# Second feed-forward layer: its closing row normalisation moved from two passes of its own into the loop over batches

## The reference

```python
    def _L1_ffn_ref(x, Wr, br, W1, b1, W2, b2, gamma, beta):
...
        h = jax.nn.gelu(jnp.einsum('nd,edf->enf', xf, W1) + b1[:, None, :], approximate=False)
        y = jnp.einsum('enf,efd->end', h, W2) + b2[:, None, :]
        w_dense = jnp.zeros((N, E), x.dtype).at[jnp.arange(N)[:, None], top_i].add(top_w)
        out = jnp.einsum('ne,end->nd', w_dense, y).reshape(B, S, D)
        out = _layer_norm(out + x, gamma, beta)
        return out
...
    x = x + _L1_ffn_ref(_layernorm(x, axis=-1), L1_ffn_Wr, L1_ffn_br, L1_ffn_W1, L1_ffn_b1, L1_ffn_W2, L1_ffn_b2, L1_ffn_gamma, L1_ffn_beta)
    x = x + _L2_gnn_ref(_layernorm(x, axis=-1), adj, L2_gnn_W1, L2_gnn_b1, L2_gnn_W2, L2_gnn_b2)
```

## Time and profile before

| | |
|---|---|
| median of 3 runs | 6786.41 us (6783.37 to 6788.06) |
| the profiled execution: its own time | 6792.14 us |
| the profiled execution: span in the trace | 6790.4 us |
| busy over the span | PE 79%, DVE 67%, ACT 34%, POOL 1% |
| batch loop of the layer, 4878.4 to 5004.0 us of the span | PE busy all through |
| statistics of YB, 5004.0 to 5026.9 us | VectorE, one turn to ScalarE |
| closing pass over the batches, 5026.9 to 5082.8 us | VectorE alone |

### The profile page before, as it was taken

How to read it: one execution, slowest core, us unless ns; L and a number is a source line. 1 busy time by engine, 2 the same in 40 slices (tenths; PEclk the granted TensorE clock), 3 DMA queues, 4 the chain that set the end, 5 groups by cost and what they waited for, 6 DMA issues and landing times. The chain is left out here.

```text
span 6790.4 us, 109815 instructions
## 1 busy us (share of the span) xinstructions
PE 5355.4 (79%) x33047; PEld 3803.4 (56%) x33047; DVE 4564.6 (67%) x27007; ACT 2311.9 (34%) x7369; POOL 93.6 (1%) x128
## 2 busy tenths in 40 slices
PE   4666788888877769969899976993546699776999
PEld 4555566666666534446566653662333477554676
DVE  7888888888888853379999997775562333424333
ACT  1222222222222235449599881110110233201333
POOL 0000000000000000000000000000000000000000
PEclk9999999999999999969999987996778799876999
DMA  1000000000000000010000000000000000000000
GB/s 46 2 2 2 2 3 5 3 4 4 4 4 3 4 21 13 7 54 6 6 4 6 4 3 8 1 1 0 25 28 0 13 0 0 9 0 13 0 0 25
DMA packets 27823, 56.57 MB, mean 8 GB/s; under 512 B 6186, under 2 KB 16835, under 8 KB 25539
## 3 DMA queue, kind: packets, MB, share of 16 engines
q1 hardware_dynamic: 27330, 50.79, 2.2%
HBM read 38.20 MB, written 12.58 MB: 7 GB/s over the span
## 5 line engine op out<-in xcount | busy, mean ns | idle before, releaser
L2007 DVE SCALAR_TENSOR_TENSOR f_ACC<-f_yp,f_CG,f_ACC 128x128 f32<-128x128 f32 x1024 | 288.4, 344 | 461.6 <-DVEq L2005 461.6
L1952 PEld LDWEIGHTS f_yp<-f_W,f_hs 128*128 128x128 f32 x4096 | 490.0, 192 | 92.6 <-issue 91.8
L1886 PE MATMUL f_hp<-f_rows,f_W 128*128 128x512 f32 x1024 | 531.5, 602 | 5.1 <-ACT U L1896 3.0
L1054 ACT ACTIVATE e_XD<-e_X,e_scal 128x60 f32<-128x60 f32 x2048 | 527.5, 333 | 17.5 <-DVEq L918 15.7
L710 PE MATMUL h_small<-h_part,ones 128*128 128x2 f32 x1024 | 300.6, 363 | 294.3 <-DVE h_jd L579 198.4
L1983 ACT ACTIVATE f_hs<-f_hp,f_b 128x512 f32<-128x512 f32 x512 | 347.7, 685 | 539.7 <-ACTq L1982 539.7
L655 ACT ACTIVATE h_VW<-h_v,h_s 128x8 f32<-128x8 f32 (+3 forms) x512 | 154.8, 302 | 1082.6 <-DVE h_s L417 1082.6
L1942 PE MATMUL f_hp<-f_XT,f_W 128*128 x1024 | 484.4, 601 | 33.0 <-PEq L2236 33.0
L703 PEld LDWEIGHTS h_ax<-h_XM,h_parts 128*128 128x128 bf16 x11520 | 480.8, 114 | 40.9 <-issue 40.9
L1952 PE MATMUL f_yp<-f_W,f_hs 128*128 128x128 f32 x4096 | 493.5, 275 | 0.0
L710 PEld LDWEIGHTS h_small<-h_part,ones 128*128 128x128 f32 x1024 | 256.6, 311 | 415.0 <-DVE h_jd L579 287.6
(11 more groups left out here) (716 smaller groups left out, 11363.2 us busy)
## 6 DMA issues: line engine op xcount, KB each, us to landing
f_S<-in_f_W SPq DMA_DIRECT2D x64, 128.0 KB, 2.3
X<-in_x SPq DMA_DIRECT2D x1, 4096.0 KB, 16.3
held<-g0e_HL SPq DMA_DIRECT2D x16, 256.0 KB, 2.0
g_HL<-held SPq DMA_DIRECT2D x16, 256.0 KB, 2.8
f_W<-in_f_W SPq DMA_DIRECT2D x2, 2048.0 KB
spill<-f_xts SPq DMA_DIRECT2D x16, 256.0 KB, 2.0
f_rows<-spill SPq DMA_DIRECT2D x16, 256.0 KB, 2.7
f_W<-in_f_W SPq DMA_DIRECT2D x4, 1024.0 KB
```

What stands on the lines that cost most here:

```text
L1054: ins = nc.scalar.activation(XD[b][:, k, h, :], X[:, :], ACT.Identity, bias=scal[b][:, k, 2 * h:2 * h + 1])
L1886: nc.tensor.matmul(self.hp[s % 3][:, :], self.W1[:, e, j * P:(j + 1) * P], self.rows[:, g % 2, :], start=True, stop=True).then_inc(self.h_ ...
L1952: ins = nc.tensor.matmul(yp[:, u % 2, k, :], hs[:, u % 2, c, k * P:(k + 1) * P], W2[:, u * UC + c, :], start=(c == 0), stop=(c == UC - 1))
L2007: ins = V_.scalar_tensor_tensor(ACC[:, k, :], yp[:, u % 2, k, :], CG[:, k * E + e:k * E + e + 1], ACC[:, k, :], ALU.mult, ALU.add)
```

## The change

The two closing stages go. Their work moves into `chosen_experts`:

- VectorE takes bn_stats of a batch's four YB tiles directly after writing them, and adds beta to X's rows of the batch directly after the batch's input rows were normalised.
- Mean and variance become scales in two halves of 32 tiles, batches 0 to 7 (FIRST = 8) and 8 to 15. VectorE's `variance(half)` comes at the end of batch 7 and after the loop; ScalarE's `deviation(half)` (a square root) after its Gelus of batch 8 and after the loop; VectorE's `scales(half)` in batch 9 and after the loop.
- The normalising itself moves to ScalarE: `finished_rows(g)` makes YN = YB * rstd + bias with four instructions on 128x128, each with a scale and a bias that are one value per row. VectorE's `scaled_rows(g)` multiplies by gamma and adds to X. Both run nine batches behind (BEHIND = 9): batches 0 to 6 inside the loop's batches 9 to 15, and batches 7 to 15 after the loop.

```diff
+        YN = sb("YN", [P, 2, GT, D])
...
+        FIRST, BEHIND = 8, 9
+        halves = (slice(0, FIRST * GT), slice(FIRST * GT, T))
...
+                def finished_rows(g):
+
+                    act.wait_ge(bias_in, 1 if g < FIRST else 2)
+                    if g >= 2:
+                        act.wait_ge(x_out, g - 1)
+                    for k in range(GT):
+                        t = g * GT + k
+                        nc.scalar.activation(YN[:, g % 2, k, :], YB[:, t, :], ACT.Identity, scale=prstd[:, t:t + 1],
+                                             bias=pbias[:, t:t + 1]).then_inc(yn_full, 1)
+
+                def deviation(half):
+
+                    act.wait_ge(var_in, half + 1)
+                    nc.scalar.activation(psd[:, halves[half]], pv[:, halves[half]], ACT.Sqrt).then_inc(sd_out, 1)
...
+                    if g == FIRST:
+                        deviation(0)
+                    if g >= BEHIND:
+                        finished_rows(g - BEHIND)
+                deviation(1)
+                for g in range(B - BEHIND, B):
+                    finished_rows(g)
...
+                def variance(half):
...
+                    dve.wait_ge(stat_in, T // 2 * (half + 1))
...
+                def scales(half):
...
+                    dve.wait_ge(var_in, half + 1)
+                    dve.wait_ge(sd_out, half + 1)
...
+                def scaled_rows(g):
+
+                    dve.wait_ge(yn_full, GT * (g + 1))
+                    xs = X[:, g * GT:(g + 1) * GT, :]
+                    V_.tensor_tensor(YN[:, g % 2], YN[:, g % 2], gm[:, :].unsqueeze(1).broadcast_to([P, GT, D]), ALU.mult).then_inc(ch2, 1)
+                    dve.wait_ge(ch2, done.next())
+                    V_.tensor_tensor(xs, xs, YN[:, g % 2], ALU.add).then_inc(x_out, 1)
...
                     V_.tensor_tensor(ACC[:, a], XG[:, a], bp[:, a, 0:D].unsqueeze(1).broadcast_to([P, GT, D]), ALU.add).then_inc(y_free, 1)
+                    xs = X[:, g * GT:(g + 1) * GT, :]
+                    V_.tensor_tensor(xs, xs, bt[:, :].unsqueeze(1).broadcast_to([P, GT, D]), ALU.add).then_inc(ch2, 1)
+                    done.next()
                     dve.wait_ge(y_free, 3 * g + 1)
+                    if g == FIRST + 1:
+                        scales(0)
...
+                    for k in range(GT):
+                        V_.bn_stats(st[:, g * GT + k, :], YB[:, g * GT + k, :]).then_inc(stat_in, 1)
+                    if g == FIRST - 1:
+                        variance(0)
+                    if g >= BEHIND:
+                        scaled_rows(g - BEHIND)
+                variance(1)
+                scales(1)
+                for g in range(B - BEHIND, B):
+                    scaled_rows(g)
+                dve.wait_ge(x_out, B)
...
-        if post:
-            statistics(nc, C, signal, YB, mean, rstd, name + "_post")
...
-                                normalize(nc, dve, ch3, done, xg, YB, mean, rstd, g * GT, GT).then_inc(ch3, 1)
...
-                                V_.tensor_tensor(xg, xg, gm[:, :].unsqueeze(1).broadcast_to([P, GT, D]), ALU.mult).then_inc(ch3, 1)
...
-                                V_.tensor_tensor(xg, xg, bt[:, :].unsqueeze(1).broadcast_to([P, GT, D]), ALU.add).then_inc(ch3, 1)
...
-                                V_.tensor_tensor(xs, xs, flat(xg), ALU.add).then_inc(ch3, 1)
```

More of the change, by code:

```diff
@@ L2034, in chosen_experts @@
         ACC = sb("ACC", [P, 2, GT, D])
+        YN = sb("YN", [P, 2, GT, D])
+        st = sb("post_st", [P, T, 6])
+        pa, pb, pv, psd, pmean, prstd, pbias = (sb("post_" + k, [P, T]) for k in ("a", "b", "v", "sd", "mean", "rstd", "bias"))
         hp = bctx.enter_context(nc.psum_tensor(f"{name}_hp", [P, 2, FC, S], F32))
@@ L2090, in _ @@
                 done = Count()
+                def variance(half):
+                    hv = halves[half]
+                    dve.wait_ge(stat_in, T // 2 * (half + 1))
+                    me, mo, qe, qo = st[:, hv, 1], st[:, hv, 4], st[:, hv, 2], st[:, hv, 5]
+                    V_.tensor_tensor(pb[:, hv], me, mo, ALU.subtract).then_inc(ch2, 1)
+                    dve.wait_ge(ch2, done.next())
+                    V_.tensor_tensor(pa[:, hv], qe, qo, ALU.add).then_inc(ch2, 1)
+                    done.next()
+                    V_.scalar_tensor_tensor(pb[:, hv], pb[:, hv], 0.25, pb[:, hv], ALU.mult, ALU.mult).then_inc(ch2, 1)
+                    dve.wait_ge(ch2, done.next())
+                    V_.scalar_tensor_tensor(pv[:, hv], pa[:, hv], 1.0 / D, pb[:, hv], ALU.mult, ALU.add).then_inc(ch2, 1)
+                    dve.wait_ge(ch2, done.next())
+                    V_.tensor_scalar(pv[:, hv], pv[:, hv], EPS, None, ALU.add).then_inc(var_in, 1)
+                    V_.tensor_tensor(pmean[:, hv], me, mo, ALU.add).then_inc(ch2, 1)
+                    dve.wait_ge(ch2, done.next())
+                    V_.tensor_scalar(pmean[:, hv], pmean[:, hv], 0.5, None, ALU.mult).then_inc(ch2, 1)
+                    dve.wait_ge(ch2, done.next())
@@ new lines, in scales @@
+                def scales(half):
+                    hv = halves[half]
+                    dve.wait_ge(var_in, half + 1)
+                    dve.wait_ge(sd_out, half + 1)
+                    V_.reciprocal(prstd[:, hv], psd[:, hv]).then_inc(ch2, 1)
+                    dve.wait_ge(ch2, done.next())
+                    V_.tensor_tensor(pa[:, hv], prstd[:, hv], prstd[:, hv], ALU.mult).then_inc(ch2, 1)
+                    dve.wait_ge(ch2, done.next())
+                    V_.tensor_tensor(pa[:, hv], pa[:, hv], pv[:, hv], ALU.mult).then_inc(ch2, 1)
+                    dve.wait_ge(ch2, done.next())
+                    V_.tensor_scalar(pa[:, hv], pa[:, hv], -0.5, 1.5, ALU.mult, ALU.add).then_inc(ch2, 1)
+                    dve.wait_ge(ch2, done.next())
+                    V_.tensor_tensor(prstd[:, hv], prstd[:, hv], pa[:, hv], ALU.mult).then_inc(ch2, 1)
+                    dve.wait_ge(ch2, done.next())
+                    V_.scalar_tensor_tensor(pbias[:, hv], pmean[:, hv], -1.0, prstd[:, hv], ALU.mult, ALU.mult).then_inc(bias_in, 1)
@@ L2102, in _ @@
                         dve.wait_ge(y_free, 3 * g + 2 + c)
+                    for k in range(GT):
[9 more added lines that the diff above has]
+                dve.wait_ge(x_out, B)
+                dve.wait_ge(ch2, done.n)
 def experts(nc, C, X, w, name, F, func, by_batch=False, affine=False, post=False):
@@ L2366, in experts @@
         if by_batch:
-            chosen_experts(nc, C, signal, X, XT, XG, mean, rstd, w, b2, CBT, BS, index, share, YB, name, F, func)
+            chosen_experts(nc, C, signal, X, XT, XG, mean, rstd, w, b2, CBT, BS, index, share, YB, gm, bt, name, F, func)
         else:
             all_experts(nc, C, signal, X, XT, W1, W2, b1, b2, CB, name, F, func)
-        if post:
-            statistics(nc, C, signal, YB, mean, rstd, name + "_post")
[L2372 to L2383, removed]
-                                normalize(nc, dve, ch3, done, xg, YB, mean, rstd, g * GT, GT).then_inc(ch3, 1)
-                                dve.wait_ge(ch3, done.next())
-                                V_.tensor_tensor(xg, xg, gm[:, :].unsqueeze(1).broadcast_to([P, GT, D]), ALU.mult).then_inc(ch3, 1)
-                                dve.wait_ge(ch3, done.next())
-                                V_.tensor_tensor(xg, xg, bt[:, :].unsqueeze(1).broadcast_to([P, GT, D]), ALU.add).then_inc(ch3, 1)
-                                dve.wait_ge(ch3, done.next())
-                                xs = X[:, ds(g * GT, GT), :].rearrange("p a b -> p (a b)")
-                                V_.tensor_tensor(xs, xs, flat(xg), ALU.add).then_inc(ch3, 1)
-                                added = {**(added if b else {}), b: done.next()}
-                            dve.wait_ge(ch3, done.n)
-                            dve.sem_clear(ch3)
 GT = 4
```

5 lines of the change are left out of this document (4 added, 1 removed).

## The result

The changed kernel took 6714.85 us (median of four executions, 6713.43 to 6719.67), the kernel before 6787.24 (6783.37 to 6789.85).

A forecast was written before the change was run, and what follows sets the result against it. TensorE was taken to bound the batch loop and VectorE the closing pass. With the loop costing nothing more, 58.8 us off the profiled 6792.14 gave 6733.3, less 5.73 for the median: 6728 us, range 6717 to 6741.

The forecast's parts named there:

- the bound on the clock: Next stage's first matmuls: a shift in where TensorE's clock rises may change the time by 1.5 us either way.
- The layer's gain: Behind the loop: 78.8 us shrink as X's last row ends at 5024.0 instead of 5082.84, 58.8 us won.
- The table changes: ScalarE's square-root loads, 1.28 us each: covered in batch 9 by 0.3 us, on the path behind the loop.
- The rival by the Trainium skill: Each table switch adds a drain of some 1380 ns; 2.5 us more in all, 6730 us. Chance 0.06.
- ScalarE's group: Four 128x128 normalising instructions with two per-row operands: 1.26 us a group, one instruction every 0.29 us.
- the upper bound: ScalarE's four normalising instructions without overlap: 0.49 us each, 1.96 us a group, 4.5 us more in the tail.
- The rival in which ScalarE paces the tail: Nine groups behind the loop at 1.96 us each on ScalarE, 17.6 us, 4.5 more; 6732 us. Chance 0.13.
- The tail's total: From the loop's last row at 5004.02 to X's last row at 5024.0, with nine groups taking 13.1 us.
- VectorE as the loop's bound: VectorE above 7.62 us a batch, say 8.6 in the last seven; 7 us come back, 6735 us. Chance 0.07.
- The side of slower: TensorE's clock falls in the loop, a batch taking 15.2 us; with all 16 batches 6850 us. Chance 0.03.
- the rivals that made the gain smaller: ScalarE pacing the tail (6732 us, 0.13), a drain per table change (6730, 0.06), VectorE bounding the loop (6735, 0.07).

The follow-up runs named there:

- after_w8: Changed kernel with one VectorE operation of 8 columns (0.17 us) added behind its last row; executions 6717.60, 6717.81, 6733.90 and 6736.51 us.
- load_behind: Changed kernel with a one-column ScalarE copy, waiting for the variance, ahead of each square root; 6716.69, 6731.96, 6733.48 and 6735.54 us.
- rows_on_dve_warm: Changed kernel with YB's normalising moved from ScalarE to VectorE, plus six unread matmuls in each closure round of the fourth graph layer; 6716.76 us.
- after_d1: Changed kernel with one 128x512 VectorE operation (0.73 us) added behind its last row; 6732.26 us.
- after_again: The changed kernel itself, unedited, in four more executions; 6715.31, 6718.65, 6727.36 and 6729.58 us.
- no_scale: Changed kernel with the per-row scale left out of ScalarE's YN instructions, so its output is not the reference's; 6716.26 us.
- after_d2: Changed kernel with two 128x512 VectorE operations (1.46 us) added behind its last row; 6730.46 us.
- after_w1024: Changed kernel with one VectorE operation of 1024 columns (1.2 us) added behind its last row; 6734.50 us.
- quarters: Changed kernel with statistics in four parts of four batches instead of two of eight, finishing five batches behind instead of nine; 6723.53 us.
- before_d2: Kernel before with two 128x512 VectorE operations (1.46 us) added behind its closing pass; 6791.45 us.
- before_d3: Kernel before with three 128x512 VectorE operations (2.19 us) added behind its closing pass; 6793.15 us.

## Why the prediction was wrong

- **The step that failed** is the bound on the clock: "where the clock rises among them may shift by a few of them, so 1.5 us either way at the next stage", and, with it, that a later stage's length changes is something "which nothing here gives cause for". The runs showed a later stage whose TensorE clock takes one of two courses: its rounds took 65.9 us before and 51.2 after, 12.1 us of the kernel's time, and executions of one kernel lie up to 19 us apart (after_w8). 58.8 us off the kernel before gave 6728. In its eight executions the changed kernel had 6727.4 and 6729.6 on what by their times is the slow course, which is the forecast to within 2 us, and 6713 to 6720 on the fast one; that all four executions of the result were fast ones was luck. The sign was in the trace before: these rounds had a granted clock of 0.67, though TensorE waited only 2.35 us in each. The sum never asked what they would take at full clock, since no edit was near.
- **The layer's gain**: forecast 58.8, measured 59.7 (landmarks) and 59.3 (with the clock's choice gone). What was forecast of the loop held: 7.62 us a batch, the first weighted row on time. VectorE's busy time in the loop was 83.2 us, not "near 87": a batch's eight rows took 5.97 us together, not 6.6, since they overlap a little.
- **The table changes** cost nothing. In the loop the sum had the reload start when batch 9's first Gelu was due and make it 1.28 us late. It ran earlier, at 4941.42, while ScalarE would have waited for hp, and that Gelu came on time (4944.02, 7.62 us after the one before). Behind the loop the sum had the load on the path, 1.3 us too much: the last load ran at 4994.54, before the variance was out, and only the square root behind it waited for that, at 5000.47. load_behind puts the load on the path and gets 1.5 us. The earlier trace rows had shown it behind the wait; in that code a semaphore clear stands between the wait and the square root and in the changed kernel nothing does, but whether that is the reason was not tried. The rival by the Trainium skill (ScalarE: Activation LUTs, "What ACT_TABLE_LOAD costs", a drain of some 1380 ns with each switch) is not borne out here: 0.02 us from the load's end to the square root, and 0.01 us from the last Gelu of batch 8 (4938.98 + 0.69) to the load ahead of it (4939.68).
- **ScalarE's group** was put at 1.26 us and took 1.64, so a group came every 1.6 us in the tail and not every 1.46. From the last scale (5002.31) to the end of X's last row are 14.3 us, where the sum has 13.1: 1.2 us more. A single instruction lasts 0.48 us, as the upper bound had it (0.49), but the instructions overlap, which the upper bound (1.96 a group) left out. The rival in which ScalarE paces the tail is what happened, with about a quarter of its 4.5 us. The sum also lacks ScalarE's time for the first of the nine groups. That was free for a reason that it doesn't give: group 7 belongs to the first half, so ScalarE began it at 5000.61, 1.7 us before the last scale was ready.
- **The tail's total** (19.3 us against 20.0) is near by luck: the load's 1.3 us too much and the groups' 1.2 us too little nearly cancel.
- **VectorE as the loop's bound** didn't come, not even with 1.1 us more a batch (rows_on_dve_warm). The side of slower: the clock in the loop stayed at 0.98.

What sets the course is settled in part. Counted from the first matmul of the first round, the granted clock of the first 0.8 us and of 4.3 to 6.5 us is this, in the changed kernel and in after_d1:

```profile
5985.70:5986.50 0.80, 0.80 (x7) 0.80 (x8) 0.00 (x0) 0.80 (x1) 0.00 (x0) 1.00 0.00 0
5990.00:5992.20 2.20, 1.99 (x10) 1.41 (x8) 0.07 (x1) 0.00 (x0) 0.00 (x0) 1.00 0.00 0
```

```profile
5990.71:5991.51 0.80, 0.80 (x4) 0.80 (x4) 0.00 (x0) 0.80 (x1) 0.00 (x0) 0.50 0.00 0
5995.01:5997.21 2.20, 2.20 (x6) 1.72 (x6) 0.00 (x0) 0.00 (x0) 0.00 (x0) 0.50 0.00 0
```

after_again and no_scale have the 1.00 and 1.00 of the fast course too. after_d2, after_w8, after_w1024, load_behind and quarters have 0.50 and 0.50 with the slow one, before 0.55 and 0.50; before_d2 and before_d3 have 0.68 and 1.00, and the 64.3 us. So the first round tells the course: the later the clock falls in it, the fewer of the rounds behind it are slow. This is an order read from one profile of each kernel, and no run set that moment on purpose. Open is what sets it, and with it the odds. One and the same kernel has both courses, so it isn't the kernel's instructions alone; a phase against something that doesn't start with the kernel would fit, and wasn't tested.

## What to carry to other kernels

Work moved under an engine that fills its stage was free here while the sum of the engine that took it stayed below the period, and the timeline says so in its waits: VectorE went from 3.3 us a batch to 6.0, and in rows_on_dve_warm to 7.0, of 7.62 without a loss. What remains is the part behind the last row, so shorten that part, not the work: statistics in parts of four batches instead of eight gave 6 us more. And before a difference is put down to an edit, hold landmarks of both traces side by side; here a loop in which TensorE waits 2.35 us a round was worth 12 us by its clock, more than any of the rivals that made the gain smaller (7 us at most), and a few matmuls in the wait, which nobody reads, settled it.

## What the runs showed of the hardware

- The same rounds took 65.9 us at a granted clock of 0.67, 51.2 at 0.88, and 45.2 at 1.00 with six matmuls more in each. Adding matmuls that nobody reads made the kernel before 19 us faster (6767.42 against 6786.95).
- A ScalarE instruction of 128x128 between SBUF tiles lasts 0.48 us with a per-row scale and a per-row bias, and four take 1.64; with the bias alone four take 1.27.
- The square root's table load (1.28 us) ran 5.9 us ahead of the square root (4994.54, 5000.47), while only the square root waited for the variance. With a one-column copy behind the wait (load_behind) the load ran behind the copy, and the stretch was 1.50 us longer.
- Rounds with 2.35 us of waiting for TensorE in each can have their clock fall in every round (0.50 in the first 6.2 us of its matmuls, 10.3 us a round) or in none of several (1.00, 7.0 us a round).
